# TensorE's step 5: the key projection of the second attention moved behind the first attention's applied values

## What is computed

```python
x = x + window_attention(group_norm(x))      # 16 heads of 32, windows of 8 x 8, shifted
t = tokens(x)
t = t + attention(layer_norm(t))             # 8 heads of 16, over the 256 tokens of an image
t = t + mixture_of_experts(layer_norm(t))    # 8 experts, the 2 best of each token
```

## Time and profile before

| | |
|---|---|
| median of 3 runs | 781.23 us (781.10 to 782.13) |
| the profiled execution's own time | 778.79 us |
| its span | 777.0 us |
| TensorE busy (matmul) | 649.7 us, 84% |
| TensorE weight loads | 550.2 us, 71% |
| VectorE busy | 515.8 us, 66% |
| ScalarE busy | 506.4 us, 65% |
| GpSimd busy | 483.8 us, 62% |
| mean granted TensorE clock, as a share of full speed | 0.945 |

### The profile page before, as it was taken

The page is one execution under the profiler, slowest core; times in us unless marked ns, Lnnn a source line. Parts: engine busy times, 40 slices in busy tenths (PEclk is TensorE's granted clock), DMA queues, the critical chain, the costliest instruction groups (busy, mean ns, idle before and its releaser), DMA issues. The chain is left out here.

```text
span 777.0 us, 20293 instructions
## 1 busy us (share of the span) xinstructions
PE 649.7 (84%) x7070; PEld 550.2 (71%) x7070; DVE 515.8 (66%) x1513; ACT 506.4 (65%) x1427; POOL 483.8 (62%) x556
## 2 busy tenths in 40 slices
PE   3987999998988989889898988987784799999900
PEld 2766878787877778777777877766663688888800
DVE  5666767778778777888778887784442356565612
ACT  3555888878877778878778887665550166766600
POOL 6354656665767677677766767567465336666644
PEclk8698999999999999999999999999998699999965
DMA  7002013031230313313133130321642213232257
GB/s 211 19 3 35 11 27 84 23 90 31 79 98 20 96 33 87 76 41 100 34 86 77 40 101 25 88 50 73 183 143 96 63 49 93 87 92 87 69 143 209
DMA packets 54218, 59.27 MB, mean 76 GB/s; under 512 B 10370, under 2 KB 49410, under 8 KB 53602
## 3 DMA queue, kind: packets, MB, share of 16 engines
q1 hardware_dynamic: 44918, 45.65, 22.9%
q0 software_dynamic: 4544, 9.38, 3.4%
q10 hardware_dynamic: 4656, 2.95, 1.4%
HBM read 36.00 MB, written 28.64 MB: 83 GB/s over the span
## 5 line engine op out<-in xcount | busy, mean ns | idle before, releaser
L566 POOL TENSOR_TENSOR pb<-pb,rcb 128x512 f32<-128x512 f32 x128 | 155.5, 1215 | 155.5 <-DVE rcb L859 154.2
L614 POOL DMA_INDIRECT ysl<-yo,dst x78 | 75.4, 967 | 59.1 <-DVE yo L1133 42.4
L725 ACT ACTIVATE pb<-pSB,mxb 128x256 f32<-128x256 f32 x128 | 59.6, 470 | 47.2 <-DVE mxb L959 46.6
L574 POOL TENSOR_TENSOR pa<-pa,rca 128x512 f32<-128x512 f32 x64 | 67.3, 1051 | 29.0 <-DVE rca L1024 29.0
L1252 PE MATMUL pTB<-ident,pb 128*128 128x128 f32 x512 | 80.0, 279 | 5.4 <-ACT ptb L739 5.4
L725 ACT ACTIVATE pb<-pSA,mxb 128x256 f32<-128x256 f32 x128 | 59.7, 476 | 35.1 <-DVE mxb L959 35.1
L739 ACT ACTIVATE ptb<-pTB 128x512 f32<-128x512 f32 x128 | 77.2, 603 | 1.6 <-PE pTB L1252 1.6
L500 POOL DMA_INDIRECT slots<-rec,slot x64 | 65.3, 1020 | 13.8 <-issue 13.6
L745 ACT ACTIVATE pta<-pTA 128x512 f32<-128x512 f32 x64 | 38.5, 601 | 45.5 <-PE pTA L1339 45.4
L1252 PEld LDWEIGHTS pTB<-ident,pb 128*128 128x128 f32 x512 | 58.6, 142 | 9.1 <-issue 7.1
L959 DVE TENSOR_REDUCE mxb<-pSB 128x2 f32<-128x512 f32 x64 | 43.9, 686 | 21.4 <-PE pSB L1221 21.4
(11 more groups left out here) (221 smaller groups left out, 2027.1 us busy)
## 6 DMA issues: line engine op xcount, KB each, us to landing
slots<-sel_dram SPq DMA_DIRECT2D x16, 1040.0 KB
kbd<-kst SPq DMA_DIRECT2D x128, 64.0 KB, 2.4
xt<-slots SPq DMA_DIRECT2D x39, 130.0 KB, 2.2
xch<-x_ch_dram SPq DMA_DIRECT2D x4, 512.0 KB, 6.9
xt<-x_tok_dram SPq DMA_DIRECT2D x16, 128.0 KB, 2.4
xch<-t SPq DMA_DIRECT2D x16, 128.0 KB, 2.0
fw<-f_dram SPq DMA_DIRECT2D x1, 2048.0 KB, 9.0
yc<-ysl SPq DMA_DIRECT2D x8, 256.0 KB, 9.5
```

The lines of the kernel that those rows point to most:

```text
L566: pool.tensor_tensor(pb[:, b, :, :], pb[:, b, :, :], rcb[:, b, :].unsqueeze(2).to_broadcast([128, 2, TOK]), ALU.mult).then_inc(sb_nrm, 1)
L574: pool.tensor_tensor(pa[:, u, :, :], pa[:, u, :, :], rca[:, b, :].unsqueeze(2).to_broadcast([128, 8, WIN]), ALU.mult).then_inc(sa_nrm, 1)
L614: pool.indirect_dma_start(ysl, bass.IndirectOffsetOnAxis(ap=dst[:, t % YB, n:n + 1], axis=0), yo[:, t % YB, n, :], None).then_inc(y_dma[t ...
L725: last = a.activation(pb[:, b, qc, :], (pSB, pSA)[n % 2][:, qc * TOK:(qc + 1) * TOK], ACT.Exp, bias=mxb[:, b, qc:qc + 1], accum_out=smb[:, ...
```

## The change

In PE's step 5 the key projection goes behind the applied values of the first attention. The query projection of step 6 stays where it was. Both keep their waits and their signals; no other engine's list is changed.

```diff
-                    if M is not None and n in (5, 6):
-
-                        if n == 5:
-                            pe.wait_ge(m_lo, M.j + 1)
-                            if M.j == 0:
-                                pe.wait_ge(c_w1l, 1)
-                        else:
-                            pe.wait_ge(m_klo, M.j + 1)
+                    if M is not None and n == 6:
+
+                        pe.wait_ge(m_klo, M.j + 1)
                         for g in range(2):
-                            c = (QK1 if n == 5 else 0) + g * 128
+                            c = g * 128
                             mm = split_product(pM[:, g * TOK:(g + 1) * TOK], w1h[:, c:c + 128], w1l[:, c:c + 128],
                                                t1h[:, :], t1l[:, :])
-                        mm.then_inc(m_k if n == 5 else m_q, 1)
+                        mm.then_inc(m_q, 1)
                     for J, u in applied(A, M, n):
...
                         mm.then_inc(oa_mm, 1)
+                    if M is not None and n == 5:
+
+                        pe.wait_ge(m_lo, M.j + 1)
+                        if M.j == 0:
+                            pe.wait_ge(c_w1l, 1)
+                        for g in range(2):
+                            c = QK1 + g * 128
+                            mm = split_product(pM[:, g * TOK:(g + 1) * TOK], w1h[:, c:c + 128], w1l[:, c:c + 128],
+                                               t1h[:, :], t1l[:, :])
+                        mm.then_inc(m_k, 1)
```

## The result

| | before | after |
|---|---|---|
| median of 13 runs each, taken by turns | 779.27 us (776.39 to 782.13) | 773.36 us (769.30 to 776.89) |
| the profiled execution's own time | 778.79 us | 776.03 us |
| its span | 777.0 us | 774.2 us |
| its mean granted TensorE clock | 0.945 | 0.953 |

The ratio of after to before, taken round by round, is 0.9912, with a 95% interval from 0.9892 to 0.9932 (5.3 to 8.4 us less); the two medians are 5.9 us apart. Predicted were 778.7 us, a ratio of 0.9968. The sign was right, and the size and the range were wrong. The median of before was 781.23 us with the three runs known then and is 779.27 us with thirteen, so 2.0 of the 5.3 us between forecast and result are the base. The other 3.4 us are a gain that was put too low: 5.9 us measured against 2.5.

What follows compares the result with a forecast made beforehand. No engine was full; TensorE was busiest (84%), its largest relevant wait the keys' 17.5 us for `t1l`. Terms 0 x 15, +0.1 and -2.6 gave -2.5 us: 781.23 to 778.7 us, range 776.0 to 782.0.

Steps and rivals of the forecast that it cites:

- The move in a full iteration: Step 5: applied values run inside TensorE's stall for `t1l`, keys start unchanged, head 6's scores 0.62 us earlier; iteration gain 0.
- The early iteration: One early iteration with only 0.36 us of stall for `t1l`: keys about 0.2 us late, loss taken as 0.1 us.
- The clock: TensorE's clock, halved behind the longest stalls for `t1l` in full iterations, was to stay full after the change: 2.6 us gained.
- two falls, so 2.6 us: Two falls of TensorE's clock in the full iterations, costing 1.28 and 1.30 us, were both expected to go.
- one long stall speaks against so simple a reading: A 1.79 us stall, in the first iteration with no image left in G, had no clock fall behind it.
- the keys' chain is where it was: From keys through eight DMAs to head 0's scores: unmoved, 10.27 us as before, so no gain there.
- the freed 0.62 us gets through: Rival at the value projection: DVE's L924 comes earlier, 0.17 us in 14 iterations, 2.4 us more, 776.3 us; chance 0.09.
- The sum: Whole kernel: 0 x 15 for steady iterations, +0.1 us for the early one, -2.6 us for the clock: -2.5 us.
- keys late: Rival: past 0.21 us, keys, their DMAs and head 0's scores move; 0.2 us in 15 iterations, 784.2 us; chance 0.08.
- The base: The whole kernel's median of 781.23 us, 2.4 us above the profiled execution, from which the forecast took 2.5 us.

Runs made afterwards that it cites:

- new_order_held: The changed kernel with three added matmuls (0.65 us together) behind the key projection, so head 6's scores start where they did before; 774.12 us, ratio 0.9929.

## Why the prediction was right and wrong

**The move in a full iteration: right.** Forecast were the applied values 0.15 us behind `t2`; they start at 346.04, and `t2` ends at 345.89. The keys are 0.05 us behind the end of `t1l` as before, and head 6's scores 0.82 us behind the keys' start (about 0.9 forecast, 1.53 before). `tn2` waits 0.25 us and the value projection 0.54, both forecast as longer. One detail was missed: applied group 2 was to wait longer than its 0.30 us and waits 0.24, since it waits for ScalarE, which comes earlier itself; it starts 0.38 us earlier, not 0.25. The gain of the iteration is 0.01 us.

**The early iteration: right, and smaller than its term.** The keys come 0.64 us behind the start of `t1l` instead of 0.47, so 0.17 us late (0.2 forecast). The iteration takes 31.65 us instead of 31.63; the term was 0.1 us.

**The clock: right in kind.** No fall is left from 120 to 515 us in any profile of the new order, where the old one has 10 in six profiles up to 545 us. The rule of the Trainium skill that frequent short idle times between matmuls make the clock swing (TensorE: Matmul & The Clock Gate, "A second HAM failure mode: psum-queue depth-cycling") spoke against it. This case doesn't bear it out: the stall is cut into pieces of 0.73 and 0.15 us and more come behind it, and the clock stays at 2.4 GHz there in five profiles of the changed kernel. It isn't proof against a fall: with matmuls added to the new order there is one in three profiles, at 521.9 us in `new_order_held`.

**The clock: the count rested on one execution.** The step "two falls, so 2.6 us" counted one profile. Six profiles show 0 to 3 falls in the full iterations, 1.2 in the mean, and in three of them one more at the 15th. The step "one long stall speaks against so simple a reading" took a chance for a property: that iteration fell in three profiles of six. By count the term is 10 falls x 1.28 / 6 = 2.1 us, so it was put a little too high and isn't where the missing gain lies. That it came out near 2.6 is luck in part: the one profile had two falls, and another would have given none or three. The runs' clocks allow more: 11.5 us less at half clock on the first chip and 77.5 - 68.7 = 8.8 on the fourth, 2.0 and 1.5 us at the rate of 0.17, 4.3 and 3.3 at that of 0.375. The start has 18 us at half clock in the mean of before and 12 in that of after, but is only 0.6 us shorter.

**The step that failed: "the keys' chain is where it was", in one iteration of three.** It holds for where the DMAs begin (+3.29 and +3.28 us) and not for their landing where instructions are loaded at the same time. This step, priced at 0, measured 1.0 us: 1.80 against 0.76 us of waits. The rival "the freed 0.62 us gets through" priced such a gain at 2.4 us and named the value projection, which didn't move.

**The sum has no term outside of the full iterations.** It put the start at nothing without a reason. The start is 0.6 us shorter in the mean, but it differs by 3.5 us among five profiles of the same kernel, so this isn't told from chance.

**The rival "keys late": its price was too high in full iterations.** It put 0.2 us per iteration on any delay past 0.21 us. Keys 0.81 us late cost 0.3 us in a steady iteration; its direction was right, and the change itself doesn't come near the point, with 0.15 us of wait left.

**The base.** The sum was put under a median of three runs, 2.0 us above that of thirteen. The prediction left open why that median lay 2.4 us above the profiled execution; the median of thirteen lies 0.5 us above it, and the runs scatter by 6 us. The upper end of the range, too, is off its own sum: 781.3 and 0.9 are 782.2, not 782.0.

**Still open.** The difference of the first comparison is 5.9 us, with an interval from 5.3 to 8.4; on the first and the fourth chip it is 5.3 and 4.3. The stages ahead of the experts account for 3.9 us: 2.1 for falls, 1.0 for waits, 0.6 in the start, the rest small. Between 0.4 and 2.0 us of the gain are thus without a cause that is shown. The scatter between profiles of one kernel is large enough to hide them (from the 3rd to the 15th `t1l` alone it is 1.8 us), and so is that of the experts' stage and the end, 157.9 to 161.6 us in the profiles of the first chip, which the stages leave out. The clocks of before's runs in the first comparison aren't known. That a later packet would make the wait longer still, or a much earlier one remove it, wasn't tried.

## What to carry to other kernels

A stall that ends in the same place costs nothing more for being there, but behind a long one TensorE's clock can fall: put work that is ready, or else matmuls that nobody reads, inside it, and make sure that the instruction which ends it isn't made late. Count such falls over several executions before pricing them, and don't price the mean clock of whole runs by what one fall costs in one place: here the two rates were 0.17 and 0.375 us per us at half clock. Work added to an engine's list also moves where its instructions are loaded, so a kernel with added work differs from its twin in more than the stall. Where an iteration waits for many small DMAs, look at whether some other queue, instruction loading included, has a packet among them.

## What was not expected of the hardware

- The loading of instructions, in packets of 16 KB, delays small DMAs beside it: the keys' last landing goes from 10.2 to 10.7 us behind the start of `t1l` to 10.6 to 11.6, and moves with how early TensorE is in its list.
- The same stall (1.79 us in the 15th iteration, 1.4 to 1.85 us in others) is followed by a fall of the clock in some executions and not in others of the same kernel: 0 to 3 falls in the full iterations.
- The time of one and the same kernel differs by chip: 779.70, 786.76 and 787.23 us, mostly in the stage of the experts (116.6 us in the first profile of before, 124 to 134 in those of the second and third chip).
